# A fused conv-gate and routed-FFN kernel on one core: the later batches' statistics and gates go through DRAM, and the program around them is reordered

## The reference, cut to what matters

```python
# x: 8 images, 512 channels, 16 x 16 pixels
x = x + conv(ln_c(x))                   # ln over the channels of each pixel
t = tokens(x)                           # 2048 tokens of 512
t = t + ffn(ln_t(t))
def conv(x):                            # one gate for each image and channel
    u = stack([mean, max, std(ddof=1)]) over the 256 pixels
    med = median(u.reshape(b, -1))      # over the 1536 numbers of one image
    g = sigmoid(einsum((u - med) ** 3, cfc_w) / sqrt(1 + eps) * bn_w + bn_b)
    return x * g
def ffn(x):                             # top 1 of 8 experts, plus a shared one
    logits = x @ router_w.T; w = sigmoid(top value)
    out = w * glu(x, expert chosen) + glu(x, shared)
# glu(x) = silu(x @ wg) * (x @ wu) @ wd, all 512 x 512, fp32
```

## Time and profile before

| | |
|---|---|
| runs | 403.72, 403.89, 403.95 us |
| the profiled execution | 403.9 us, of which its span (first to last instruction) 402.1 us |
| PE busy | 381.4 us, 95% of the span |
| DVE, ACT, POOL busy | 253.5, 158.4, 137.1 us |
| DMA | 55.96 MB, mean 139 GB/s |
| mean granted TensorE clock | 0.988 of full speed |

### The profile page before, as it was taken

One profiled execution on the slowest core, in us unless ns is written; L12 is line 12 of the kernel. 1 busy time (PEld: TensorE's weight loads), 2 busy tenths in 40 slices (PEclk: granted clock), 3 DMA queues, 4 the chain that ended last, 5 costly groups with the idle time before them and its releaser, 6 DMA issues.

```text
span 402.1 us, 6788 instructions
## 1 busy us (share of the span) xinstructions
PE 381.4 (95%) x1974; PEld 304.2 (76%) x1977; DVE 253.5 (63%) x489; ACT 158.4 (39%) x270; POOL 137.1 (34%) x195
## 2 busy tenths in 40 slices
PE   5857799999999999999999999999999999999994
PEld 2422588887888888888888888888888888888883
DVE  6888876745665676779864477375275655676222
ACT  3875655456321124331124353163355315363110
POOL 6689332300000111024120344435334442545211
PEclk9988999999999999999999999999999999999998
DMA  8900140101115322533140768545646862753200
GB/s 310 416 11 0 52 132 27 52 30 50 54 52 187 129 79 79 184 131 98 61 132 26 266 233 309 197 130 214 229 171 237 291 234 80 270 186 92 79 28 30
DMA packets 14764, 55.96 MB, mean 139 GB/s; under 512 B 2575, under 2 KB 2575, under 8 KB 11280
## 3 DMA queue, kind: packets, MB, share of 16 engines
q1 hardware_dynamic: 9936, 40.93, 28.4%
q0 software_dynamic: 4800, 14.69, 10.3%
HBM read 43.02 MB, written 13.63 MB: 141 GB/s over the span
## 4 chain that ended last, share of the span: by engine, by line
PE 87%; DVE 4%; ACT 4%; POOL 2%; issue 1%; DMA 1%; DVEq 0%; POOLq 0%; ACTq 0%
PE GU L1507 48%; PE yb L1507 24%; PE th L1499 4%; PE tx L1492 4%; PE th L1536 2%; PE th L1363 1%; ACT x_sb L594 1%; DMA x_sb<-x_tok 1%; PE mb L1507 1%; ACT scratch L612 1%; DVE tok_parts L843 1%; ACT scratch L608 1%; PE yb L1544 0%; ACT w_parts L627 0%; PE GU L1432 0%
## 5 line engine op out<-in xcount | busy, mean ns | idle before, releaser
L1507 PE MATMUL GU<-w_parts,xT 128*128 (+1 forms) x864 | 214.2, 396 | 0.2 <-DVE xT L1078 0.2
L1507 PEld LDWEIGHTS GU<-w_parts,xT 128*128 128x128 f32 x864 | 158.2, 188 | 31.5 <-DVE xT L1078 0.4
L1507 PE MATMUL yb<-w_parts,hT 128*128 (+1 forms) x420 | 102.8, 393 | 0.0
L1507 PEld LDWEIGHTS yb<-w_parts,hT 128*128 128x128 f32 x420 | 77.7, 188 | 15.6
L661 ACT ACTIVATE hT<-th 128x512 fp32r<-128x512 f32 x36 | 21.5, 598 | 159.3 <-PE th L1499 159.3
L534 POOL DMA_INDIRECT out<-x_sb,scatidx x20 | 36.9, 1844 | 93.1 <-DVE x_sb L1296 80.7
L1069 DVE TENSOR_TENSOR w_parts<-w_raw,w_parts 128x2048 f32 (+1 forms) x24 | 54.9, 2287 | 6.8 <-issue 6.6
L1053 DVE TENSOR_TENSOR hidden<-hidden,GU 128x512 f32<-128x512 f32 x36 | 24.7, 687 | 36.0 <-PE GU L1507 35.9
L584 ACT ACTIVATE w_parts<-w_raw 128x2048 f32 (+1 forms) x24 | 45.2, 1910 | 4.2 <-issue 4.0
L1047 DVE TENSOR_TENSOR hT<-th,hT 128x512 fp32r<-128x512 f32 x36 | 24.8, 688 | 27.7 <-ACT hT L661 27.5
L497 POOL TENSOR_TENSOR x_rstd<-x_mv,eps 128x1 f32<-128x1 f32 x16 | 3.1, 192 | 95.8 <-DVE x_mv L1017 95.8
(11 more groups left out here) (277 smaller groups left out, 340.6 us busy)
## 6 DMA issues: line engine op xcount, KB each, us to landing
w_raw<-weights SPq DMA_DIRECT2D x27, 1024.0 KB, 5.3
x_sb<-x_tok SPq DMA_DIRECT2D x8, 512.0 KB, 8.1
xn_d<-tiles SPq DMA_DIRECT2D x16, 256.0 KB, 2.0
z_d<-x_sb SPq DMA_DIRECT2D x16, 256.0 KB, 2.2
tiles<-xn_d,tokidx POOLq DMA_INDIRECT x20, 4.7
x_sb<-z_d,tokidx POOLq DMA_INDIRECT x20, 5.5
out<-x_sb,scatidx POOLq DMA_INDIRECT x20, 6.7
conv<-conv_par SPq DMA_DIRECT2D x1, 10.0 KB, 6.7
```

The costliest lines, as they stand in the source:

```text
L1507: last = pe.matmul(dst, left[:, lp, kc, :], wset(q, k, wp, kc), start=(i == 0), stop=(i == 3 * KC - 1))
```

## The change

It has these parts.

1. The head: all four batches' token statistics come first on DVE and POOL. The channel means of batches 0 to 2 (second half) are made by PE (`mean_chunks`: four matmuls of a block of `x_sb` with a column of -1/256) and copied by ACT (`keep_means`, 128x2) in place of ACT's two passes. Batch 2 gets banks of its own. `last_std` makes its power in two halves, and DVE does the second half's scaling. Fewer `keep_warm` matmuls.
2. POOL: of the 12 low parts only 8 are made in one burst; two (DOWN) wait for `z_ready`, two come behind `rstd_tile(2)`.
3. `turn_batch(4)` moves ahead of the first product, into `yb` in place of `mb`; ACT's `channel_squares(4)` moves ahead of `token_norm(5)`.
4. The second group's statistics are written by SP to DRAM (`stats_d`) and read back, spread over partitions. `turn_planes`, `keep_V` and three spreading copies are gone; the slices are 48 wide in place of 128.
5. The gates of batches 5 to 7 are written to `gates_d` and read back spread, in place of three `spread_gate`.
6. Logits are turned four tiles at a time (`TURNS`: passes 2, 6, 9 and the last).
7. `scatter(b)` now waits for all earlier scatters (one semaphore `o_out`), `stored` is gone, and the nine tests at the end are one wait.

```diff
@@ SP
+            def spread_second_values():
+                sp.wait_ge(means_kept, 5)
+                sp.wait_ge(std_done, B)
+                sp.wait_ge(bank_measured, 2 * B)
+                sp.dma_start(stats_d.rearrange("b (p s) -> p b s", p=P), stats_f[:, group(1), :]).then_inc(stats_out, 16)
+                sp.wait_ge(stats_out, 16)
+                sp.wait_ge(wlo, 2)
+                for b in range(GROUP):
+                    sp.dma_start(V_second[b * TPART:(b + 1) * TPART, :], stats_d[b:b + 1, :].to_broadcast([TPART, NV])).then_inc(values_in, 16)
+                sp.dma_start(slices_second, stats_d.rearrange("b (r s) -> (b r) s", r=TPART)).then_inc(values_in, 16)
+            def spread_later_gates():
+                sp.wait_ge(g_ready, 2)
+                sp.dma_start(gates_d.rearrange("b (k p) -> p b k", p=P),
+                             gates[:, LOADED_GATES.start:LOADED_GATES.stop, :],
+                             allow_slow_non_contiguous=True).then_inc(gates_out, 16)
+                sp.wait_ge(gates_out, 16)
+                sp.wait_ge(x1_ready, 2 * GROUP)
+                for b in LOADED_GATES:
+                    i = b - LOADED_GATES.start
+                    sp.dma_start(gate_rows(b), gates_d[i:i + 1, :].to_broadcast([P, C])).then_inc(gates_in, 16)
             for n in range(NT):
+                if n == 2:
+                    spread_second_values()
+                if n == SECOND_SET_IN:
+                    spread_later_gates()
@@ POOL
-            for k in range(3):
+            for k in (GATE, UP):
                 for kc in range(KC):
+                    low = first_lo(k, kc)
                 low.then_inc(wlo, 1)
+            pool.wait_ge(z_ready, 1)
+            first_lo(DOWN, 0)
+            first_lo(DOWN, 1)
...
             rstd_tile(2, 2)
+            first_lo(DOWN, 2)
+            first_lo(DOWN, 3).then_inc(wlo, 1)
@@ scatter
+                if b:
+                    pool.wait_ge(o_out, 16 * b)
                 pool.wait_ge(y_used, NT + b + 1)
-            for b in range(NT - 1, NB):
-                with pool.If(needed == b + 1):
-                    stored(b)
+            pool.wait_ge(o_out, needed * 16)
@@ ACT
+            def keep_means(b):
+                act.wait_ge(means_by_pe, b + 1)
+                act.activation(neg_mean[:, b, :], yb[:, 2 * b:2 * b + 2], ACT.Copy).then_inc(means, 2)
@@ PE
+            def mean_chunks(b):
+                if b:
+                    pe.wait_ge(means, 2 * b)
+                for k in range(2):
+                    for h in range(2):
+                        last = pe.matmul(yb[:, 2 * b + k:2 * b + k + 1], x_sb[:, 2 * b + h, (2 + k) * P:(3 + k) * P], share[:, :],
+                                         start=(h == 0), stop=(h == 1))
+                last.then_inc(means_by_pe, 1)
-            def turn_logits(n, bank):
-                for i, t in enumerate(routed_in(n - 1)):
-                    pe.wait_ge(logits_kept, t + 1)
-                    pe.transpose(bank[:, i * 2 * E:(i + 1) * 2 * E], logits_T[:, t % 2, :], ident[0:2 * E, 0:2 * E]).then_inc(logits_turned, 1)
+            def turn_logits(g, bank):
+                pe.wait_ge(logits_kept, 4 * g + 4)
+                pe.transpose(bank[:, 0:P], logits_T[:, g % 2, :], ident[:, :]).then_inc(logits_turned, 1)
@@ PE, ahead_of_up and ahead_of_down
-                if n == 2:
-                    turn_planes(0)
-                    turn_planes(1)
-                if n in GATES_IN:
-                    spread_gate(GATES_IN[n])
...
-                if n == 2:
-                    turn_planes(2)
-                    turn_planes(3)
```

More of the change, by code:

```diff
@@ L26 @@
 SEARCH_STEPS = 5
-N_CONSTS = 12
+N_CONSTS = 13
 FIELDS = 6
@@ L38 @@
 SPLIT_AFTER = (8, 9, 10)
-GATES_IN = {7: 5, 8: 6, 9: 7}
+TURNS = {2: 0, 6: 1, 9: 2}
+LAST_TURN = 3
 STORED_GATES = range(1, GROUP)
+LOADED_GATES = range(GROUP + 1, 2 * GROUP)
 SET_COL, SET2_COL, TOTAL_COL = range(3)
@@ L225, in program @@
         zg_in = [sem(f"zg_in{u}") for u in range(RING)]
-        o_out = [sem(f"o_out{u}") for u in range(RING)]
+        o_out = sem("o_out")
         router_ready = sem("router_ready")
@@ L250, in gate_rows @@
         def gate_rows(batch):
-            return scratch[:, (batch - 1) * C:batch * C] if batch in STORED_GATES else mb[:, :]
+            if batch in STORED_GATES:
+                return scratch[:, (batch - 1) * C:batch * C]
+            if batch in LOADED_GATES:
+                return scratch[:, (batch - GROUP - 1) * C:(batch - GROUP) * C]
+            return mb[:, :]
         def squared(b):
@@ L471, in last_std @@
                 b = GROUP - 1
[L472 removed]
+                pool.wait_ge(pair_measured, pairs(b))
                 own(pool.tensor_scalar(z[:, b, 0:2], bn_pair[:, b, :, 2], 1.0 / (TPB - 1), None, ALU.mult))
[L474 to L477 removed]
+                own(pool.tensor_tensor(stats[:, b, 0:2, STD], z[:, b, 0:2], powers[:, 1, 0:2], ALU.pow))
+                pool.wait_ge(last_scaled, 1)
+                pool.tensor_tensor(stats[:, b, 2:4, STD], z[:, b, 2:4], powers[:, 1, 0:2], ALU.pow).then_inc(std_done, 1)
+            for b in range(GROUP):
                 token_rstd(b)
@@ L604, in channel_squares @@
                 act.wait_ge(aT_ready, b + 1)
+                if b == 1:
+                    act.wait_ge(bank_measured, 3)
+                if b == 2:
+                    act.wait_ge(bank_measured, 6)
                 if b >= 2:
                     act.wait_ge(squares, squared(b - 2))
-                for k in range(2):
+                for k in range(2) if b >= GROUP else ():
                     act.activation(junk[:, b % 2, 0, k, :], aT[:, k, :], ACT.Copy, scale=-1.0 / TPB,
@@ L678, in _ @@
                                ACT.Copy).then_inc(xhi_half if half == 0 else xhi, 1)
-            def keep_V(i):
-                act.wait_ge(v_turned, i + 1)
-                if i == 0:
-                    act.wait_ge(wlo, 2)
-                out = slices_second if i == 3 else V_second[:, i * C:(i + 1) * C]
-                act.activation(out, (mb, GU[:, 3, :])[i % 2][:, 0:P if i == 3 else C], ACT.Copy).then_inc(v_kept, 1)
             def scan_second(i):
@@ L834, in second_bank @@
             def second_bank(b):
-                dve.wait_ge(squares, squared(b))
+                if b in (1, 2):
+                    dve.wait_ge(aT_ready, b + 1)
+                else:
+                    dve.wait_ge(squares, squared(b))
                 dve.tensor_reduce(stats[:, b, 2:4, MAX], halves(b)[1], AX_X, ALU.max).then_inc(bank_measured, 1)
@@ L880, in _ @@
             dve.wait_ge(means_kept, 3)
+            dve.wait_ge(squares, squared(last))
             dve.tensor_copy(spread_rows(0, KC, 2 * KC), stats_plane(0, MEAN)).then_inc(spread_ready, 1)
@@ L1379, in _ @@
                 if b < GROUP - 1:
-                    keep_warm(6 if b else 3)
+                    mean_chunks(b)
+                    keep_warm((3, 2, 4)[b])
             keep_warm(9)
@@ L1569, in _ @@
             prepare(2)
-            turn_batch(4)
             route(1, 1)
@@ L1610, in amid_down @@
                     spread_least(0)
+            routed = 2
             for n, prepared in enumerate(PREPARED):
@@ L1636, in _ @@
                     route(t, t % RING)
+                routed += len(held + first)
             def rank():
```

175 lines of the change are left out of this document (74 added, 101 removed).

## The result

The changed kernel takes 400.6 us, the median of four runs (399.93 to 401.28), beside 403.88 us for the kernel before (four runs); the ratio is 0.9919, with a 95% interval of 0.9902 to 0.9936. It is 3.3 us faster where 8.7 were forecast, and lies above the range. Its runs lie 1.35 us apart, those of the kernel before 0.23.

What follows compares the result with a forecast made beforehand. PE was taken to bound the kernel from the first product on, with the head and the end as separate pieces. 403.9 less 2.1 (head) and 6.6 (PE), end 0, gave 395.2 us; range 393.8 to 396.6.

Steps and rivals of the forecast that it cites:

- The head, 2.1 us: Ahead of the first product: 0.6 us from the statistics and 1.5 from L958, 2.1 us sooner.
- L958's 1.5 us: Head, DVE: L958 waits for POOL's burst of low parts; with a shorter burst 0.21 us for 1.69.
- the statistics' 0.6: Head: mean passes leave ACT, POOL is late next, ACT's spreading copy starts sooner; 0.6 us, bounds 0 and 2.2.
- PE, 6.6 us: PE behind the first product: transposes and logit turns taken away save 6.6 us together.
- The term of the logits: Pass loop on PE: fewer turns of logits save 3.0 us, bounds 1.0 and 4.0.
- The gates' write: SP's write of gates ahead of tile 10's mixing: lands in 3 us, bounds 2 and 24, hidden in its slack.
- PE waits as long: Late transfers: PE loses the time by which they are late; for the gates' 24 us landing, 12.5 us.
- That rival's 7 us: Clock rival, first products: about 7 us at half clock take 3.4 us more, 398.6 us; chance 0.04.
- The values: Second group's values for the first scan: in between 84.9 and 87.4 us; cost 0, up to 1.5 us.
- late values: Rival at the first scan: it starts 1 to 3 us behind and PE waits, 396.2 to 398.5 us; chance 0.13.
- The gates as the slower rival: Rival at tile 10: gates' write takes 24 us, PE waits 12.5, 407.7 us; decides from about 20; chance 0.04.
- The end, 0: Last scatter: one wait gains 0.6 us, a start 0.5 later cancels it; 0, with 0.6 either way.

Runs made afterwards that it cites:

- the means alone go back: Mended kernel with the head's channel means of batches 0 to 2 made by ACT's two passes again, without PE's matmuls for them: 395.97 us.
- the low parts alone: Kernel before the change with only POOL's split of the 12 low parts (8 in the burst, two and two later): 402.47 us.
- the mended kernel: Changed kernel with three edits: gates written as 12 rows, second group's statistics written ahead of tile 1's store, last scatters free of earlier ones: 395.15 us.
- the doubled write: Changed kernel with the write of the gates issued twice, the second behind the landing of the first: 411.83 us.
- the kernel with free scatters: Changed kernel with the wait for earlier scatters moved ahead of the gather, so the last scatters wait for none: 400.36 us.
- the kernel with sooner statistics: Changed kernel with the second group's means copied ahead of batch 7's last maximum and the statistics written ahead of tile 1's store: 399.62 us.
- the kernel with one read: Mended kernel with the second group's values read by one DMA in place of four, the slices' read off the first scan's wait: 401.01 us.

## Why the prediction was wrong, point by point

- **The head, 2.1 us: right.** 1.97 in the trace, and 1.2 to 2.1 over all executions with this head. L958's 1.5 us are 1.45 when made alone, the statistics' 0.6 are 0.5 in the trace (and 0.8 when the means alone go back). The working of the 0.6 doesn't add up as written: 16.9, two times 1.35 and 1.8 make 21.4, not 21.7; POOL is done at 21.80. The reason given for L958, a wait for the end of POOL's burst, is borne out: with a burst of 8 that is over at 34.1 in the changed kernel, and at 35.2 in the one with the low parts alone, it takes 0.21 us.
- **PE, 6.6 us: right in size.** Between the first product and DVE's last result 1.2 us are gone in the changed kernel, where 6.6 were to go; with both transfers mended the rest is gone too. The term of the logits was 3.0 and is 2.7; the gates' 1.3 is 1.2 (with 0.1 paid for the new transpose). The sum of all terms, 395.2, is what the mended kernel measures (395.15), and that agreement is in part luck: in its trace the head gives 1.35 for 2.1 and the end 0.57 for 0, and PE's 6.6 are what is left after 0.1 for a transpose and 0.4 of waiting.
- **The gates' write: the step that failed.** "Its 1536 runs of 4 bytes have no like in the trace ... I take 3: the transfers of 80 or 128 bytes in the load of x did not show." It lands in 11.7 us. The bounds of 2 and 24 held it; the value between them was chosen by transfers that had other work to hide in, and for which no row gives a landing of their own. In the trace its packets are over 2.3 us behind the issue, and 9.4 us follow. The slack was well sized: 9.5 + 2 for the write and 3.5 for the reads, 15.0 in all; the trace has 14.6 before PE waits and 17.1 us of write and reads. The three reads took 5.4 from the first issue to the last landing, with weight loads issued behind them, and not 3.5. So the wait has two parts: with a write of 3 the slower reads would have been hidden, and with reads of 3.5 this write would have left PE waiting for 0.6 us and not for 2.5 (an estimate by these sums).
- **The price of a wait: left out.** "PE waits as long" was the rule for every late transfer. The trace has 2.5 us of waiting and a loss of 1.6 at the lower clock behind it, and the doubled write says that this doesn't grow with the wait. The clock stood among the rivals for the head only. That rival's 7 us at the low level don't follow from the row it names: 0.80 over 10 us are 4 us.
- **The values, "Taken: 0, with up to 1.5 us": the second step that failed.** They were in at 83.9, or 87.3 on the prediction's scale (3.4 us later, by SP's store before it), at the late end of its 84.9 to 87.4 and behind the "about 86" from which PE was to wait. PE waits 1.2 us more than before. So two of the rivals' mechanisms came true at once, late values and a late write of the gates.
- **The gates as the slower rival.** The mechanism named there was the right one, with a landing of 24 for 11.7 and a point of decision (about 20) that only asked when the kernel gets slower than before, not when it loses the gain.
- **The end, 0: right in its parts.** The scatter starts 0.54 later (forecast 0.5) and the end comes 0.64 sooner behind it (forecast 0.6).

## What to carry to other kernels

Work taken from the bounding engine and given to a DMA pays only if the whole round trip (write, landing, issues, reads) fits its slack: start the write when its data is there, give it few long runs (one transpose made 1536 into 12), and take the late end of the bounds for an access pattern that the trace has not shown. PE's wait, where it was otherwise never idle, is to be priced at its length and the clock behind it: here 1.6 to 3.1 us for waits of 2.2 us and more, nothing for waits of up to 1.8. Terms counted as instructions at their traced cost between the same neighbours came out within some tenths here; those of a transfer of a new shape did not, and their upper bound belongs in the range.

## What the runs showed of the hardware

- A write of 6 KB from SBUF to DRAM in 1536 runs of 4 bytes lands in 11.0 to 11.8 us (five executions), issued again at once in 8.9; in 12 runs of 512 bytes in at most 1.75 us. Its packets are over some 2.3 us behind the issue; the rest, 9.4 us in the changed kernel and 6.7 in the second write, the DMA engines are all but idle.
- PE's wait at tile 10 is followed by work at 1.2 GHz: behind 2.5 us of waiting the loss was 1.6 us, behind 2.2 us (the kernel with free scatters, where the level falls only in the product behind the wait, 4.55 us for 2.97) 1.7, behind 2.9 us (the kernel with sooner statistics, 4.94 us for 2.97) 3.1, and behind 12.9 us 1.8; behind the 5.0 us in the kernel with one read it was 2.1. The waits in pass 3 of 0.24 to 1.8 us left the granted clock at 1.00.
- A DVE instruction of 0.2 us with two SBUF inputs waited 1.5 us for the end of a row of POOL instructions, 1.23 us each, though it started in the middle of one. The one just ahead of it (L957), with one input in PSUM, took 0.20 us inside the same row. The Trainium skill, "SBUF — State Buffer", section "Who interferes with whom", has DVE and GpSimd share a port pair under an exclusive lock, held for one instruction. If that is what L958 waits for, the row before the change has the lock pass from one of POOL's instructions to the next; the runs themselves show only that the wait ends with the row.
- One DMA of 768 KB whose source has 4 as its slowest dimension lands in over 12 us, four DMAs of 192 KB in about 4 from the issue of each.
- The kernels with the changed head and with transfers in this chain spread over 0.4 to 4.2 us from run to run (the statistics' kernel from 397.62 to 401.81; the mended one and those made from it with four reads over 0.4 to 0.8), the kernel before and the one that differs from it by the low parts alone over 0.2 to 0.4.
